# Mixer order: where the two halves of the second norm stand in a quad's tiles

## The reference

```
x = x + attn_a(layernorm(x))   # gated state scan: 8 heads, state 128, rotation by a cumulated angle
x = x + ffn(layernorm(x))      # receptance * (relu(k)^2 @ W_v), with a shift by one token
x = x + attn_b(layernorm(x))   # projection, short filter, long convolution over the sequence
x = x + ffn(layernorm(x))

layernorm(x) = (x - mean) / sqrt(var + 1e-5)
ffn: xr = mu_r*x + (1-mu_r)*x_prev;  xk = mu_k*x + (1-mu_k)*x_prev
     out = sigmoid(xr @ W_r.T) * (relu(xk @ W_k.T)^2 @ W_v.T)
```

## Time and profile before

| | us |
|---|---|
| median of 3 runs | 4547.78 |
| lowest, highest | 4546.89, 4550.72 |
| the profiled execution | 4551.91 |
| its span, first to last instruction | 4550.2 |
| TensorE busy in the span | 4199.4 |
| VectorE | 3223.3 |
| ScalarE | 2217.5 |
| GpSimd | 1855.1 |

### The profile page before, as it was taken

One profiled execution on the slowest core, in us unless ns is written; L12 is line 12 of the kernel. 1 busy time (PEld: TensorE's weight loads), 2 busy tenths in 40 slices (PEclk: granted clock), 3 DMA queues, 4 the chain that ended last, 5 costly groups with the idle time before them and its releaser, 6 DMA issues. The chain is left out here.

```text
span 4550.2 us, 119987 instructions
## 1 busy us (share of the span) xinstructions
PE 4199.4 (92%) x40212; PEld 3406.1 (75%) x40212; DVE 3223.3 (71%) x6736; ACT 2217.5 (49%) x5180; POOL 1855.1 (41%) x2776
## 2 busy tenths in 40 slices
PE   5389999999999999999999999999859999989999
PEld 3167777777777777777777777777648888878888
DVE  8757767777677776777767777767636666658888
ACT  3235444444444444444544445444436666645555
POOL 3345445444454444444444444445300000026666
PEclk9699999999999999999999999999979999989999
DMA  8320111111111111111111111111046666633333
GB/s 277 115 93 30 49 38 37 51 39 46 39 39 51 39 37 48 39 45 43 38 49 39 40 47 39 49 37 38 31 119 182 179 179 187 180 100 105 104 105 95
DMA packets 380370, 352.30 MB, mean 77 GB/s; under 512 B 26585, under 2 KB 353113, under 8 KB 370777
## 3 DMA queue, kind: packets, MB, share of 16 engines
q1 hardware_dynamic: 362972, 328.71, 24.2%
q10 hardware_dynamic: 16896, 16.78, 1.1%
HBM read 235.94 MB, written 109.44 MB: 76 GB/s over the span
## 5 line engine op out<-in xcount | busy, mean ns | idle before, releaser
L753 PE MATMUL bank<-w_bc,xnT 128*128 128x512 f32 x3072 | 837.0, 416 | 15.3 <-POOL xnT L1096 15.1
L965 ACT COPY turned_t<-bank 128x512 f32<-128x512 f32 x512 | 300.1, 586 | 915.5 <-PE bank L776 915.5
L753 PEld LDWEIGHTS bank<-w_bc,xnT 128*128 128x128 f32 x3072 | 583.3, 198 | 160.3 <-issue 45.6
L1498 PE MATMUL p_yc<-sig,toep 64*64 64x256 f32 (+14 forms) x16384 | 543.3, 283 | 16.0 <-issue 12.3
L1498 PEld LDWEIGHTS p_yc<-sig,toep 64*64 64x64 f32 x16384 | 480.0, 133 | 92.4 <-issue 46.1
L1104 POOL TENSOR_TENSOR turned_b<-rot 128x512 f32<-128x512 f32 x256 | 326.7, 1276 | 537.2 <-DVE rot L1203 537.2
L1202 DVE TENSOR_TENSOR rot<-bank,par 128x512 f32<-128x512 f32 x512 | 350.2, 684 | 256.4 <-issue 120.1
L1291 DVE SCALAR_TENSOR_TENSOR conv<-bank,short,conv 128x511 f32<-128x511 f32 (+1 forms) x384 | 286.7, 747 | 113.5 <-ACT conv L1026 99.3
L1104 POOL TENSOR_TENSOR turned_c<-rot 128x512 f32<-128x512 f32 x256 | 344.0, 1344 | 38.9 <-DVE rot L1203 38.9
L1203 DVE TENSOR_TENSOR rot<-bank,par 128x512 f32<-128x512 f32 x512 | 347.7, 679 | 0.0
L880 PE MATMUL bank<-x2T,in_w 128*128 128x512 f32 x1152 | 315.1, 410 | 18.8 <-issue 9.2
(11 more groups left out here) (270 smaller groups left out, 9353.5 us busy)
## 6 DMA issues: line engine op xcount, KB each, us to landing
toep<-taps_dram SPq DMA_DIRECT2D x256, 260.0 KB, 4.2
el<-el_dram SPq DMA_DIRECT2D x256, 128.0 KB, 3.0
xg<-arg_x SPq DMA_DIRECT2D x32, 512.0 KB, 4.7
xnT_dram<-xt_g ACTq DMA_DIRECT2D x32, 512.0 KB, 3.9
xnT_raw<-xnT_dram SPq DMA_DIRECT2D x128, 128.0 KB, 2.4
x_quad<-arg_x SPq DMA_DIRECT2D x32, 512.0 KB, 3.7
x_dram<-x_quad SPq DMA_DIRECT2D x32, 512.0 KB, 2.9
x0T_dram<-conv SPq DMA_DIRECT2D x32, 512.0 KB, 2.8
```

Of the source, the lines that this page charges most:

```text
L753: last = mm(p_bc[c][:, :], xnT[w.q % 2][p][:, k, :], w_bc[q][:, k, c * 1024 + g * W4:c * 1024 + (g + 1) * W4], start=(n == 0), stop=(n == ...
L965: s_.copy(turned_t[g][c][:, :], p_tr[:, :]).then_inc(s[f"copy_{BC[c]}"], 1)
L1498: last = mm(by_seq(p_y[p][c][odd * H:(odd + 1) * H, 0:2 * TILES])[:, :, first:], toep[n % SLOTS][c * H:(c + 1) * H, lag * H:(lag + 1) * H] ...
```

## The change

The first half of the second norm moves to the last tile of the iteration before (q == 3 with `quad(1, ...)`), on all three engines. The second half moves within the first tile into the place that the first half had. On VectorE in the last tile, the residual stands behind the fourth `rotate` and ahead of `carry_state`; on GpSimd, the scalars stand behind the last `add_turned` and ahead of the scalars of the first norm's first half; on ScalarE, the normalisation stands behind `copy_state`, at the end of the tile.

```diff
@@ ScalarE @@
                     if q == 0:
-                        quad(2, normalised, 2, 0)
+                        quad(2, normalised, 2, 1)
...
                     tile(q, 0, copy_turned, 0, 0)
                     tile(q, 1, copy_state)
-                    if q == 0:
-                        quad(2, normalised, 2, 1)
+                    if q == 3:
+                        quad(1, normalised, 2, 0)
...
@@ GpSimd @@
                     tile(q, 0, add_turned, 1, 1)
                     if q == 0:
-                        quad(2, layer_rstd, 2, 0)
+                        quad(2, layer_rstd, 2, 1)
                     tile(q, 0, add_turned, 1, 0)
                     if q == 0:
-                        quad(2, layer_rstd, 2, 1)
                         quad(2, before_filter)
+                    if q == 3:
+                        quad(1, layer_rstd, 2, 0)
...
                     if q == 3:
                         quad(0, layer_rstd, 1, 0)
...
@@ VectorE @@
                     tile(q, 1, weigh_gram, 1)
                     if q == 0:
-                        quad(2, residual2, 0)
+                        quad(2, residual2, 1)
...
                     if q == 3:
                         quad(1, gated, 0)
                     tile(q, 0, rotate, 1, 0)
-                    if q == 0:
-                        quad(2, residual2, 1)
+                    if q == 3:
+                        quad(1, residual2, 0)
...
                     tile(q, 1, carry_state)
                     tile(q, 2, residual1, n, q)
                     tile(q, 1, take_y, 1)
```

## The result

The changed kernel takes 4409.15 us (median of 4 runs, 4407.02 to 4410.65) against 4548.55 us before: a ratio of 0.9693, 95% interval 0.9676 to 0.9710. The forecast was 4411 us.

The account below looks back on a forecast made before the run. TensorE was taken to bound the kernel: two waits (2.57 us) and the clock fall behind them (1.97 us) cost 4.54 us a quad. Summed to 137.1 us off the profiled run, this gave 4411 us, range 4396 to 4447.

Parts of the forecast that it names:

- What bounds the kernel: TensorE, busy 92% of the span; only its waits or a slowed clock can pay.
- The two waits named: First tile, TensorE: L873 waits 1.43 us for the second normalisation, L821 1.14 us for carry_state; both go.
- The split of the 4.54 us: Per quad: 2.57 us from two TensorE waits directly, 1.97 us from the clock falling behind them.
- First tile: carry_state 3.2 us earlier, last normalisation ending at 1555.26; waits at L821 and L873 go, 2.1 and 3 us to spare.
- Last tile, VectorE: Added residual takes 3.24 us, mostly in idle time; 2.6 us cover at L821, 0.84 us before next rotation; no cost.
- Last tile, ScalarE: Added normalisation of 1.09 us leaves 0.27 us idle before copy_turned; no cost taken, up to 0.5 us a quad otherwise.
- the thinnest cover of the change: The 0.27 us of ScalarE idle time left before the next first tile's copy_turned.
- The sum: 29 quads at 4.54 us, plus 2.57 and 2.8 us: 137.1 us off the profiled 4551.91 us; less 4.1 us, 4411.
- The page on the ramp: Skill page putting the ramp penalty below 1% of span, under 45 us against 57 us: about 4423 us or more.
- The clock keeps falling: Rival: waits go, but other small gaps on TensorE lower the clock; 4430 to 4468 us, chance 10%.
- A smaller wait: Rival: copy_turned late, TensorE waits in the first tile, 0.5 to 1 us a quad; 4426 to 4441 us, chance 12%.
- Slower: Rival: last-tile residual delays carry_state, TensorE stops at L821; needs a step over 8.4 us; 4561 us, chance 3%.

Follow-up runs that it names:

- a_filler: Kernel before, with five unneeded 512-column matmuls on TensorE between the log matmul and x2n_over of the first tile: 4509.97 us, ratio 0.9910.
- a3_filler_five: Kernel before, with five unneeded 512-column matmuls on TensorE ahead of turn_state in the first tile: 4518.27 us, ratio 0.9931.
- d2_plus_3: Changed kernel, with eight more unread statistics in the moved first-half residual on VectorE in the last tile: 4435.76 us, ratio 0.9744.
- f_norm_twice: Changed kernel, with two more unread activations on ScalarE behind the moved normalisation in the last tile: 4411.74 us, ratio 0.9694.
- d3_plus_5: Changed kernel, with fourteen more unread statistics in the moved first-half residual on VectorE in the last tile: 4507.69 us, ratio 0.9916.
- c_second_late: Kernel before, with only the second norm's first half moved to the last tile, the second half left in its old place: 4465.07 us, ratio 0.9808.
- a2_filler_first: Kernel before, with four unneeded 512-column matmuls on TensorE ahead of turn_state in the first tile: 4544.32 us, ratio 0.9993.

## Why the prediction was right, point by point

**What bounds the kernel.** Right. The two waits named were the ones that went, and nothing took their place.

**The split of the 4.54 us.** The total was right (4.58 us), but that is luck in part: its two terms were mis-sized, one each way. The clock was put at 1.97 us by taking the quad from 395.63 to 489.25 us as the same work at the full clock. That quad is shorter for another reason too: after the change, with no fall anywhere, it takes 90.54 us (397.11 to 487.65) against 91.00 us on the average of the later ones. Less that 0.46 us, the clock is 1.51 us; `a_filler` gives 1.42 us, the rows from L873 to L786 1.40 us, the five quads of `a3_filler_five` 1.56 us. The waits were put at their idle time, 2.57 us; they cost 1.36 + 1.80 = 3.16 us by the windows. With 1.42 us for the clock the errors are +0.55 and -0.59 us, and nearly cancel. Why the first quad is shorter isn't shown.

**First tile.** Right. `carry_state` follows the rotation, L821 and L873 start without idle time.

**Last tile, VectorE.** Right in size and in cost: the step took 3.2 us (1482.07 less 0.17 to 1485.13), L1281 1.73 us of it, and the 2.6 us of cover at L821 were confirmed by `d2_plus_3`. The reason given for the cost of nothing behind it was not right: the 0.84 us before the next rotation were read as a wait for TensorE that absorbs the slip, but the earlier trace rows names no releaser ("issue"), and they are 0.84 us after the change too. `residual1` slips by only 0.12 us against L821 of its tile (2.81 us ahead of it before, 2.69 us after), and the slip is gone by the values' step (L1210, after L1211), ahead of that rotation. The delay that GpSimd hands to the third rotation, put at 0.3 us, is 0.36 us, taken from a wait for TensorE as foreseen (0.93 to 0.57 us).

**Last tile, ScalarE.** The idle time left, 0.27 us by forecast, is 0.30 us. But "the thinnest cover of the change" was wrong: `f_norm_twice` used it up and more at no cost. Idle time of ScalarE was read as cover of TensorE, though TensorE runs ahead of that copy.

**The sum.** The profiled run got 142.4 us faster (4551.91 to 4409.48) and the sum had 137.1. By TensorE's rows the change leads by 132.9 us at the L873 of 3186.07 us (3053.20 after), where the sum had 132.3; the 28 quads themselves gave 128.3 us, where 4.54 us each are 127.1. At the last L873 (3327.15 and 3187.17 us) the lead is 140.0 us, so the emptying pipeline gave 7.1 us, where the clock of one quad and one pair of waits, 4.8 us, were counted; 2.4 us come behind it, which the sum did not have. The medians differ by less, 139.4 us. That the forecast of 4411 us came within 2 us of 4409.15 is therefore partly luck: 4.1 us were taken off because the profiled run stood that far above the median, and they made up for most of the 5.3 us missing from the sum.

**The page on the ramp.** "TensorE: Matmul & The Clock Gate" of the Trainium skill, section "What's actually happening", puts the ramp penalty below 1% of a typical span for modelling, and I went by the rows instead. The falls of this stage cost 41 us (`a_filler`) to 45 us (29 x 1.56): just under 1%, where I had 57. But the Trainium skill says this of the warm-up, not of falls that return in every quad, and low-clock stretches elsewhere in the span aren't priced here. So the nearness of the two numbers bears out no rule.

**The rivals.** *The clock keeps falling* didn't happen: 1.00 over all 28 quads, beside 21.1 us of small gaps at L841. What the Trainium skill tells ("TensorE: Matmul & The Clock Gate", section "A second HAM failure mode: psum-queue depth-cycling"), that frequent micro-idles between groups of matmuls made the clock swing in another kernel, isn't borne out at this size of gap; `a3_filler_five` and `d3_plus_5` show the swing, some quads with and some without, at gaps of 1.4 and 1.9 us. *A smaller wait* didn't come. *Slower* needs more than an 8 us step, as `d3_plus_5` bears out.

## What to carry to other kernels

In a kernel bound by TensorE, look for the quad-wide chain on the other engines that ends in TensorE's wait, and ask which tile of the pipeline has idle time in that engine's own queue: here 3 us of VectorE's idle time in one tile took a step, and the new order saved TensorE 4.6 us in another. Price a wait from start to start against a place without it, not by the idle time shown. Idle time of a feeding engine is only a lower bound of the cover; what decides is when the bound engine needs the result.

## What the runs showed of the hardware

Work that nobody needs, put into a wait, made the kernel 41 us faster, since the granted clock then stayed at 1.00. One and the same wait of 1.43 us left the clock up in 28 quads of `c_second_late`, brought it down in 5 of 30 in `a3_filler_five`, and in 29 of 30, all but the first, with 0.25 us more beside it in `a2_filler_first`. A fall cost 1.4 to 1.6 us of time where it followed the transposes of the second norm, and about 1.0 us in `d3_plus_5`. A wait costs TensorE 0.16 to 0.37 us more than the idle time that the profile shows before the instruction. The residual's operation on x (L1280, after L1281), always 128x512, took 0.69 us where GpSimd was idle (after, at 3179.41 us), 0.93 us beside GpSimd's operations of 1.0 us in the first tile (after, at 1497.93), and 1.68 and 1.80 us where it began just behind GpSimd's `add_turned` of some 1.3 us (before, at 1549.77 and 409.78); no run here varied this by itself.
